# One result region instead of two for the scattered expert results

## What is computed

```python
x = x + jnp.tanh(g_xattn[0]) * attention(_layernorm(x), ctx_2048, ...)
x = x + jnp.tanh(g_ffn[0]) * ffn(_layernorm(x), ...)

# ffn, with x normalised
probs = softmax(x @ Wr + br); top_vals, top_idx = top_k(probs, 3); ew = softmax(top_vals)
for e in range(12):
    sel = top_idx == e
    w_e = sum(where(sel, ew, 0)) / max(sel.sum(), 1)
    h = relu(x @ w1[e] + b1[e]) @ w2[e] + b2[e]
    out = out + mask[..., None] * (w_e * h)      # mask: tokens with e among their three
pooled = out.mean(axis=1)
phi = sigmoid(relu(pooled @ Wp1 + bp1) @ Wp2 + bp2)
out = out * (1.0 - (phi > 0.7) * 0.8)
```

## Time and profile before

| | us |
|---|---|
| median of 3 runs | 2199.69 (2198.26 to 2202.16) |
| the profiled execution, its own time | 2202.73 |
| its span, first to last instruction | 2201.0 |
| second stage's first instruction on GpSimd | at 1746.3 |
| scatters (L1233) | start 1770.0 to 2159.6 |
| loads of the result regions (L1278) | issued from 2163.5, the last lands at 2181.6 |

### The profile page before, as it was taken

The page is one execution under the profiler, slowest core; times in us unless marked ns, Lnnn a source line. Parts: engine busy times, 40 slices in busy tenths (PEclk is TensorE's granted clock), DMA queues, the critical chain, the costliest instruction groups (busy, mean ns, idle before and its releaser), DMA issues. The chain is left out here.

```text
span 2201.0 us, 63903 instructions
## 1 busy us (share of the span) xinstructions
PE 2091.8 (95%) x24150; PEld 1852.5 (84%) x24150; DVE 1483.3 (67%) x3330; ACT 1306.5 (59%) x3073; POOL 805.9 (37%) x1187
## 2 busy tenths in 40 slices
PE   6999999999999999999999999999998399999994
PEld 4788888888888888888888888888887299999993
DVE  5777777777777778777777777777774433333334
ACT  2366666666666566556566666665666277777771
POOL 4333443334433334433334333334431133333331
PEclk9999999999999999999999999999999699999996
DMA  5555555555555555555555555555554394333335
GB/s 156 138 147 139 135 141 138 141 142 133 136 136 147 136 139 133 133 134 137 143 144 138 138 138 142 137 136 133 136 127 147 129 321 103 58 61 58 60 52 191
DMA packets 230672, 293.44 MB, mean 133 GB/s; under 512 B 83512, under 2 KB 156188, under 8 KB 230108
## 3 DMA queue, kind: packets, MB, share of 16 engines
q1 hardware_dynamic: 201516, 254.87, 43.7%
q0 software_dynamic: 18528, 21.64, 5.2%
q10 hardware_dynamic: 10320, 12.84, 1.8%
HBM read 104.01 MB, written 42.92 MB: 67 GB/s over the span
## 5 line engine op out<-in xcount | busy, mean ns | idle before, releaser
L647 DVE TENSOR_REDUCE max_part<-max_ps 100x1 f32<-100x512 f32 (+1 forms) x1536 | 994.6, 655 | 356.6 <-PE max_ps L951 327.1
L515 ACT ACTIVATE probs<-score_ps 128x400 f32<-128x400 f32 x1498 | 732.8, 502 | 412.2 <-PE score_ps L934 402.8
L951 PE MATMUL max_ps<-k_stack,q_stack 96*100 96x512 f32 (+1 forms) x1536 | 598.3, 390 | 15.1 <-DVE max_part L647 14.3
L934 PE MATMUL score_ps<-q_stack,k_stack 97*128 97x200 f32 (+1 forms) x2996 | 598.1, 282 | 4.1 <-ACT probs L515 3.3
L934 PEld LDWEIGHTS score_ps<-q_stack,k_stack 97*128 97x128 f32 (+1 forms) x2996 | 462.8, 183 | 69.9 <-issue 30.4
L444 POOL TENSOR_TENSOR ctx_hi<-ctx_raw,zero_col 128x256 fp32r<-128x256 f32 (+1 forms) x384 | 213.3, 587 | 466.3 <-PE v_ps L965 453.5
L1004 PE MATMUL pv_ps<-probs,v_ones 128*17 128x100 f32 x12288 | 303.4, 250 | 5.7 <-ACT pv_out L530 2.8
L1004 PEld LDWEIGHTS pv_ps<-probs,v_ones 128*17 128x17 f32 x12288 | 256.3, 98 | 51.9 <-issue 37.9
L951 PEld LDWEIGHTS max_ps<-k_stack,q_stack 96*100 96x100 f32 x1536 | 257.8, 168 | 28.1 <-DVE max_part L647 23.5
L449 POOL TENSOR_TENSOR ctx_lo<-ctx_raw,ctx_hi 128x256 fp32r<-128x256 f32 (+1 forms) x384 | 257.3, 700 | 7.5
L571 ACT ACTIVATE k_hl<-k_ps,bk_c 128x512 fp32r<-128x512 f32 (+1 forms) x192 | 127.2, 662 | 211.9 <-PE k_ps L982 190.0
(11 more groups left out here) (197 smaller groups left out, 2533.5 us busy)
## 6 DMA issues: line engine op xcount, KB each, us to landing
k_stack<-k_hl SPq DMA_DIRECT2D x496, 128.0 KB, 2.6
ctx_raw<-in_ctxT SPq DMA_DIRECT2D x64, 512.0 KB, 4.4
k_stack<-k_hl SPq DMA_DIRECT2D x496, 64.0 KB, 2.2
k_stack<-k_hl SPq DMA_DIRECT2D x252, 105.0 KB, 2.4
w_all<-in_w SPq DMA_DIRECT2D x24, 640.0 KB, 11.8
ctx_raw<-in_ctxT SPq DMA_DIRECT2D x32, 420.0 KB, 4.7
k_stack<-k_hl SPq DMA_DIRECT2D x252, 52.5 KB, 2.0
x_t<-rows_by_expert SPq DMA_DIRECT2D x86, 134.5 KB
```

The source lines that it names most:

```text
L515: act.activation(probs[0:tw, n % PROBS, :], score_bank(n)[0:tw, 0:UH * SQ], ACT.Exp, scale=SCALE).then_inc(exp_done, 1)
L647: dve.tensor_reduce(max_part[b % 2][:, h, j:j + 1], max_ps[m % 2][0:SQ, 0:CW[j]], AX.X, ALU.max).then_inc(max_read, 1)
L934: ins = pe.matmul(score_bank(n)[0:TW[i], 2 * SQ * p:2 * SQ * (p + 1)], k_stack[b % 2][:, 2 * u + p, 128 * i:128 * i + TW[i]], q_stack[b % ...
L951: pe.matmul(max_ps[m % 2][0:SQ, 0:CW[j]], q_stack[b % 3][0:96, h // 2, SQ * (h % 2):SQ * (h % 2) + SQ], k_stack[b % 2][0:96, h // 2, k0[j] ...
```

## The change

There is one result region. Every tile is added into it, so scatter t waits for the landing of scatter t - 1. One clearing DMA of ACT goes (the one at g = NT * B + 10), the offset in `slot` goes, the last stage loads five pieces instead of ten, and DVE's add of the two regions with its semaphore goes; TensorE's first matmuls of a piece wait for the load instead. Buffers (`OUT`, `SLOTBUFS`, `AHEAD`) are as they were.

```diff
-RESULTS = 2
@@ attention, SP's end and ACT
-            sp.wait_ge(res_cleared, 16 * RESULTS)
+            sp.wait_ge(res_cleared, 16)
-                if g in (NT * B, NT * B + 10):
+                if g == NT * B:
                     act.wait_ge(tail_consts, N_TAIL)
-                    act.dma_start(results[g > NT * B], zero_rows[:, 0:D].unsqueeze(1).broadcast_to(
+                    act.dma_start(results, zero_rows[:, 0:D].unsqueeze(1).broadcast_to(
                         [128, SLOTS // 128, D])).then_inc(res_cleared, 16)
@@ experts, GpSimd
             for t in range(TILES):
-                stored_by(pool, t - RESULTS)
+                stored_by(pool, t - 1)
                 pool.wait_ge(y_read, t + 1)
@@ experts, SP
             for i in range(PARTS):
-                for k in range(RESULTS):
-                    sp.dma_start(res[k][:, pieces[i], :], results[k][:, pieces[i], :]).then_inc(res_in[i], 16)
+                sp.dma_start(res[:, pieces[i], :], results[:, pieces[i], :]).then_inc(res_in[i], 16)
@@ experts, DVE
                 stored_by(dve, t - SLOTBUFS)
-                dve.scalar_tensor_tensor(slot[t % SLOTBUFS][:], no_slot[:], float(t % RESULTS * SLOTS), of_rows,
-                                         ALU.add, ALU.add).then_inc(slot_ready, 1)
+                dve.tensor_tensor(slot[t % SLOTBUFS][:], no_slot[:], of_rows, ALU.add).then_inc(slot_ready, 1)
...
             for i in range(PARTS):
-                dve.wait_ge(res_in[i], 16 * RESULTS)
+                dve.wait_ge(res_in[i], 16)
                 s = pieces[i].start
-                dve.tensor_tensor(res[0][:, pieces[i], :], res[0][:, pieces[i], :], res[1][:, pieces[i], :],
-                                  ALU.add).then_inc(res_added, 1)
-                dve.wait_ge(res_added, i + 1)
-                dve.tensor_tensor(pair_sum[:, i], res[0][:, s:s + 2, :], res[0][:, s + 2:s + 4, :],
+                dve.tensor_tensor(pair_sum[:, i], res[:, s:s + 2, :], res[:, s + 2:s + 4, :],
                                   ALU.add).then_inc(pair_ready, 1)
@@ experts, TensorE
             for i in range(PARTS):
-                pe.wait_ge(res_added, i + 1)
+                pe.wait_ge(res_in[i], 16)
```

More of the change, by code:

```diff
@@ L100, in program @@
     xs = nc.dram_tensor("rows_by_expert", [NE * REGION, XW], F32, kind="Internal").ap()
-    ys = nc.dram_tensor("results_by_token", [1 + (2 * RESULTS - 1) * SLOTS + TILES * RT, D], F32, kind="Internal").ap()
+    ys = nc.dram_tensor("results_by_token", [1 + SLOTS + TILES * RT, D], F32, kind="Internal").ap()
     x1s = nc.dram_tensor("after_attention", [B, SQ, D], F32, kind="Internal").ap()
@@ L298, in attention @@
         N_TAIL = 4
-        results = [ys[1 + SLOTS * k:1 + SLOTS * (k + 1), :].rearrange("(p i) d -> p i d", p=128)
-                   for k in range(RESULTS)]
+        results = ys[1:1 + SLOTS, :].rearrange("(p i) d -> p i d", p=128)
         def clear_pads(eng, some):
@@ L1125, in experts @@
         arena = w_all[:].rearrange("p e w -> p (e w)")
-        res = [arena[:, TPP * D * k:TPP * D * (k + 1)].rearrange("p (i d) -> p i d", d=D) for k in range(RESULTS)]
-        sums = arena[:, TPP * D * RESULTS:TPP * D * RESULTS + 3 * PARTS * D]
+        res = arena[:, 0:TPP * D].rearrange("p (i d) -> p i d", d=D)
+        sums = arena[:, TPP * D:TPP * D + 3 * PARTS * D]
         pair_sum = sums[:, 0:2 * PARTS * D].rearrange("p (i j d) -> p i j d", i=PARTS, j=2)
@@ L1169, in experts @@
         res_in = [sem(f"res_in{i}") for i in range(PARTS)]
-        res_added = sem("res_added")
         pair_ready = sem("pair_ready")
@@ L1189, in experts @@
         pieces = [slice(TPP // PARTS * i, TPP // PARTS * (i + 1)) for i in range(PARTS)]
-        results = [ys[1 + SLOTS * k:1 + SLOTS * (k + 1), :].rearrange("(p i) d -> p i d", i=TPP)
-                   for k in range(RESULTS)]
+        results = ys[1:1 + SLOTS, :].rearrange("(p i) d -> p i d", i=TPP)
         def on(t):
@@ L1207, in _ @@
             pool.memset(phi[:], 0.0).then_inc(always, 1)
-            pool.iota(spare_i[:], pattern=[[128, TILES]], base=1 + RESULTS * SLOTS,
+            pool.iota(spare_i[:], pattern=[[128, TILES]], base=1 + SLOTS,
                       channel_multiplier=1).then_inc(consts, 1)
@@ L1417, in _ @@
             for piece in outs:
-                dve.scalar_tensor_tensor(x1[:, piece, :], res[0][:, piece, :], factor[:], x1[:, piece, :],
+                dve.scalar_tensor_tensor(x1[:, piece, :], res[:, piece, :], factor[:], x1[:, piece, :],
                                          ALU.mult, ALU.add).then_inc(final, 1)
@@ L1458, in _ @@
             for i in range(PARTS):
-                pe.wait_ge(res_added, i + 1)
+                pe.wait_ge(res_in[i], 16)
                 for k in range(KD):
-                    pe.matmul(pool_ps[:, k * B:k * B + B], res[0][:, pieces[i].stop - 1, 128 * k:128 * k + 128],
+                    pe.matmul(pool_ps[:, k * B:k * B + B], res[:, pieces[i].stop - 1, 128 * k:128 * k + 128],
                               of_batch[:], start=(i == 0 and k == 0), stop=False, skip_group_check=True)
```

## The result

| us | before | after |
|---|---|---|
| median of 17 runs each, one chip | 2199.09 (2191.27 to 2203.93) | 2202.51 (2199.70 to 2210.51) |
| the profiled execution, its own time | 2202.73 | 2204.39 |
| its span | 2201.0 | 2202.6 |
| first scatter of the second stage to the last, start to start | 389.7 | 404.2 |
| last scatter's start to the end of the span | 41.4 | 32.8 |

The ratio after to before is 1.0023, 95% interval 1.0015 to 1.0031: the changed kernel is slower by 5.1 us (3.3 to 6.8), where 9.8 were forecast. The ratio is not that of the two medians, which lie 3.4 us apart. Two repeats on other chips gave 1.0044 (1.0029 to 1.0059) and 1.0022 (1.0010 to 1.0034).

A forecast was written before the change was run, and what follows sets the result against it. It took TensorE, busy for 95% of the span and 4.61 us a tile, as the bound. 2202.73 + 19 (last scatter later) - 9.4 (end) = 2212.3, given as 2209.5 us on the runs' base, 3.0 lower; range 2192 to 2225.

The forecast's parts named there:

- second clearing: The removed 3.2 MB clearing, covered by the tail of the first stage: 0, at most 1 us saved.
- Does it catch up?: Over the 72 tiles behind the `x_all` load, GpSimd's lateness shrinks by little: 3 us at 0.04 a tile.
- the link while late: Scatter start to next start while GpSimd is late: 4.6 us (4.4 to 4.9), taken as 4.57, about the period.
- The tie of DVE's copy to the landing: Past 13 us of lateness, DVE's w2 copy falls wholly inside descriptor writing, which rises to 2.0 us.
- R1: Rival: the scatter chain catches up, or early links are shorter than 8; 2192.5 us, chance 0.22.
- The quiet link of 4.3: One scatter's link in the quiet part: packets 3.6, receipt 0.44, release 0.25; 4.3 us, 0.3 under the period.
- (a): While the weights load, scatter packets are held up: four links of 8.0 us, 1770 to 1802.
- (b): One link spans the load of `x_all`, 11.5 us; GpSimd is then 20 us late.
- (c): With GpSimd late, DVE waits too and TensorE stalls about 2 us (0 to 5) at once; 18 stay as lateness.
- The end: After the last scatter, five loads replace ten and the last 1.50 us add goes: 9.4 us saved (6 to 12).
- Fetches and other stragglers: Instruction fetches now and then delay a DMA engine's scatter packets: 0.1 to 0.25 us a link, 0.1 taken.
- R2: Rival: DVE's copy shuts GpSimd out for its whole 0.83 us, or most fetches meet a scatter; 2222 to 2233, chance 0.18.

The follow-up runs named there:

- few_weights: The changed kernel with only the weights of experts 0 to 3 loaded and used for all tiles; 0.9977 of the kernel before.
- one_load: The kernel before, with the end loading region 0 alone and not adding region 1; 0.9954 of the kernel before, -10.1 us.
- chain_only: The kernel before with one edit, each scatter waiting for t - 1 instead of t - 2; 1.0052 of the kernel before, +11.4 us.

## Why the prediction was right and wrong

**Right in direction, in the link's make-up and in the end; wrong in how much the chain catches up.** The change is slower, with the last scatters late and a shorter end; the time lay in the range, and no cost of the second clearing shows. But the loss is 5.1 us where 9.8 were forecast.

**The step that failed is "Does it catch up?"**: the link while late. It was put at 4.57 us, so that of 20.2 us of delay 3 would be made good. Measured are links of 4.51, and the delay against the kernel before went from 20.4 us at scatter 8 to 12.9 at scatter 83: 7.5 us made good. The reason given for the 4.57 failed with it. The tie of DVE's copy to the landing was to keep the writing at 2.0 us and the chain late to the end. In the tie the writing is 1.79 and a link mostly 4.24 to 4.30, below the 4.35 at which the prediction let R1 win, and the chain left the tie after tile 19. What held it behind that is the lock and the stragglers. Point by point:

- The quiet link of 4.3: 3.6 to packets' end, 0.44 receipt, 0.25 release. After, links with a writing of 1.79 are 4.25 and 4.27 (1840.59, 1844.84, 1849.11 are the starts), with the landing after 4.0 of them. Right.
- (a) Four links of 8.0: 32.1 in sum for 32. Right as a sum, and few_weights shows that it is the weights. That the 8.0, a choice between 6.3 and 9.3, came out to the tenth is luck.
- (b) The link over `x_all`: 12.1 for 11.5, one tile later than placed; scatters 4 to 12 took 42.8 us where the terms give 43.6 (two of 4.6, one of 11.5, five of 4.57). Right.
- (c) A stall of TensorE of 2 us: once, where it was placed, but mis-sized. The wait is 2.8 us and TensorE lost 4.75, since the matmuls behind it ran at the half clock for a stretch. In the two repeats it lost 2.7 and 4.9. The lateness left at the last scatter, 16.6 us in the sum (18.2 - 3 + 1.4), was 9.8. So the 18.6 for 14.5 is made of one part 2.75 too small and one 6.8 too large.
- The end: 9.4 predicted, 8.6 measured. The loads did what was said: first landing 4.1 us, the last 10.4 us after the first issue for 10.2. But the term took the last load's chain as the end. With the add gone, TensorE's 1.70 us a piece (0.85 and 0.85 us at the half clock, from 2180.27 on) is longer than the loads' 1.57, which was in no row of mine, and closes the chain at 2187.11.
- "Does it catch up", the link while late: **4.57 was 4.51** in the profile (4.48 and 4.51 in the repeats). 73 x 0.06 = 4.4 us, which is about all by which the last scatter's delay was off (18.6 for 14.5). With the 0.8 at the end, which goes the other way, the +9.2 became +5.9.
- The sum itself has a small slip: 2202.73 + 19 - 9.4 less the 3.0 of the base is 2209.3, not 2209.5. It changes nothing.

The small error hides a larger one, since two of its parts were off in opposite ways. The writing was put at 2.0 us for all late links, by a ratio of cost to overlap. It is 1.74 in the mean: 1.79 in the tied state on which the 2.0 was argued, 1.55 over most of the catching up, and 2.06 only in the lock, which the prediction didn't have. Fetches and other stragglers were put at 0.1 us a link; 14 links over 4.9 us, up to 6.4, and lesser ones make it some 0.24: 73 links x (4.51 - 4.08 - 0.19), with 4.08 a link without copy or straggler and 0.19 the mean of writing above 1.55. Together 0.43 over 4.08 where 0.45 + 0.1 had been put over 4.05.

Neither "the lateness shrinks by little" nor "it catches up" is what happens: the chain gains half a microsecond a tile until it meets the copy, stays, is thrown back by 1.5 us by a straggler, and gains that again. The last tiles were still 8.6 us late.

**R1** is what the kernel without copy and loads did; the kernel without the copy alone caught up too (by tile 49), and the one without the loads had 3.1 us left. What decided against it in the changed kernel was the copy, through the lock and not through the tie, together with landings that the loads of `x_t` and, it seems, fetches lengthen and that throw the chain back. **R2**, the copy that shuts GpSimd out for all of its 0.83 us, didn't occur in the tied state (0.24). The rule of the Trainium skill, *SBUF — State Buffer*, section SBUF: two separate sides, that a copy of fp32 locks GpSimd out, fits the rows for the larger part where the copy leads (0.52 us for an overlap of 0.65, 0.25 for 0.37), and by a third only where it starts 0.88 us into the writing; there the measurement decides. The base estimate of the Trainium skill, *DMA: Bandwidth & Descriptors*, section Anatomy of one DMA — SWDGE (gpsimd) path, for such a transfer (2.3 us) is below every landing measured here (3.5 us at least, in one_load).

## What to carry to other kernels

A wait that turns two chains into one is priced by its link in the worst stretch, beside the big loads, and by how much of that the rest of the loop can make good; a spare of 0.3 to 0.5 us a tile was there and was used only in part, because at a certain phase another engine's copy took it. When two engines run with nearly the same period and one's work slows the other's, look for such a lock: the same lateness over many iterations and a link equal to the other's period. Take a sum of waits apart into what the bounding engine lost and what is still late at the end; an experiment that shortens the first can look like one that shortens the second. And price a stop of TensorE with the slower matmuls behind it: here 4.75 us for a wait of 2.8. And before ordering all scatters, ask which of them can touch the same row: here twelve of 85 can.

## What the hardware showed that was not expected

- Descriptor writing beside DVE's copy of 128 x 1280 fp32 (0.83 us) costs by phase: 0.18 us at 0.31 us of overlap, 0.25 at 0.37, 0.52 at 0.65 when the copy leads, and 0.24 when it starts 0.88 us into the writing; nothing to 0.03 us when it starts 0 to 0.5 us into it.
- A wait of 2.83 us of TensorE was followed by matmuls at a granted clock of 0.50 (1826.60 to 1829.90; 1.00 ahead of it and behind) and cost 4.75 us in all. In chain_only a wait of 4.7 us cost 7.3.
- An indirect accumulating scatter of 128 x 1 KB lands mostly 3.7 to 4.1 us after its start in quiet stretches; links of 8.0 us beside the weight loads (32.1 for four) and one of 12.1 over a single 3.2 MB load.
- Stragglers of 4.9 to 6.4 us, 14 in 73 links; an instruction fetch falls into the stretch of 13 of them, and of 11 of the other 59. In the kernel before they are hidden, since the chain there had a slack of a whole period.
